# Latent attention scores of a decoder block: from split bf16 stacks to fp32 in four row tiles, with loops written out

## The chip, the cores and the metric

The kernel runs on one core of a Trainium2 chip. The metric is the device time of one execution in microseconds (us). Before the change it is 2980.49 us, the median of 3 runs (2977.54 to 2984.96).

## The reference, cut to what matters

Three layers follow one another on x (4 batches, 1024 rows, 256 columns): a causal self attention (8 heads of 128), a cross attention over 77 context rows (16 heads of 16), and a block with a latent attention (16 heads of 16, keys and values from a 128-wide latent, causal) and a mixture of four experts, one for each row. The change concerns the scores of the latent attention:

```python
q = apply_rope((x @ Wq.T).reshape(b, t, 16, 16).transpose(0, 2, 1, 3))
latent = layernorm(x @ Wdkv.T, ln_g, ln_b)
k = apply_rope((latent @ Wuk.T).reshape(b, t, 16, 16).transpose(0, 2, 1, 3))
v = (latent @ Wuv.T).reshape(b, t, 16, 16).transpose(0, 2, 1, 3)
scores = jnp.einsum('bhqd,bhkd->bhqk', q, k) / np.sqrt(16)
scores = jnp.where(causal, scores, -jnp.inf)
attn = jax.nn.softmax(scores, axis=-1)
out = jnp.einsum('bhqk,bhkd->bhqd', attn, v).transpose(0, 2, 1, 3).reshape(b, t, 256)
```

## The kernel before, in words

Each engine has its own program, written out by hand, and semaphores tie them together. TensorE (PE) does matmuls and transposes into PSUM (8 banks of 512 f32 columns). VectorE (DVE), ScalarE (ACT) and GpSimd (POOL) work on what lies there or in SBUF; GpSimd doesn't read PSUM. SyncE (SP) loads. Every engine loops over the 4 batches (`Fori(0, BATCH)`, PE line 851, DVE 1341, ACT 635, POOL 522, SP 419); inside a batch the self attention loops over pairs of heads (line 962 on PE) and the latent attention over its 4 groups of 4 heads (`Fori(0, NG - 1)`, PE line 1210). After the batches the experts follow (from PE line 1248).

In a batch the order is: self attention, cross attention, and the latent attention, in these steps.

1. Projections. PE multiplies the turned rows by the query and latent weights (line 1088). DVE applies the rotary table to the queries (lines 1489 to 1503), ACT copies the latent columns (713), DVE and POOL normalise them, PE turns them (1095), ACT copies them (717) and PE makes keys and values (1105). DVE rotates the keys (1489 to 1512), ACT copies the values into `mv_rows` (721). While it waits PE runs matmuls of no use, `keep_warm` (823).
2. Stacks. A head has only 16 columns. To get f32 accuracy out of bf16 matmuls, query and key are split into three bf16 parts each, and six products of parts are laid side by side as a contraction of 96 rows (plus 3 rows for the maximum). ACT makes the high parts (736 to 741), DVE splits the queries (1520 to 1525), POOL the keys (557 to 561). PE turns 16 heads x 8 row tiles of each (`turn_stacks`, 1116), DVE (1564) and ACT (750) copy them out. Between the tiles, PE computes the scores of group 0 for its row maxima.
3. Maxima. For each group PE makes the 48 chunks of scores with queries in rows (`max_chunk`, 1127), each up to 512 columns, in a ring of three PSUM banks; a bf16 matmul with the identity adds the causal mask to the 32 chunks on the diagonal (1130). DVE takes the maximum of each chunk (1531). After the last chunk of the group DVE combines and splits the maxima (`stack_max`, 1540 to 1551), PE turns them (`turn_max`, 1138) and DVE and ACT write them into the last rows of the query stack (1555, 758), so that the next matmul subtracts them.
4. Keys. PE makes the scores again with keys in rows (`key_chunk`, 1152, mask 1155), also 48 chunks, in three banks; ACT takes their exponential (773) into `mprobs_t`; PE multiplies by the values (`key_products`, 1167), four heads in four column tiles of 32, f32, into banks 6 and 7; ACT copies a group's output (782). POOL copies the value columns of the group into one tile ahead (567, 572). While the keys of group g run, PE interleaves the maxima chunks of group g + 1, one for one.
5. DVE and POOL normalise the next batch's rows (1318, 1325, POOL 493 to 510), PE turns them (839), and the output projection, the gate and the routing follow.

Other lines named below: 868 and 871 are the output projection of the cross attention (four f32 matmuls of the full array, and the bias as an f32 matmul with one row), 883 the first matmul of a batch, 1365 the row maximum of the self attention.

## Time and profile before

| what | value |
|---|---|
| median of 3 runs | 2980.49 us |
| span of the profiled execution | 2933.7 us, 46553 instructions |
| the profiled execution's own time | not given apart from the runs; the span is 46.8 us under their median |
| PE busy | 2675.2 us (91%) |
| PE weight loads | 1588.7 us (54%) |
| DVE busy | 1476.0 us (50%) |
| ACT busy | 1232.9 us (42%) |
| POOL busy | 335.8 us (11%) |
| mean granted PE clock | 0.967 |

The span runs from the first to the last instruction. "Busy" is the time in which at least one instruction of the engine ran; records of PE overlap one another, as it is a pipeline. An f32 matmul shows as two records, each with its own weight load. "Issue" as a releaser means that the engine waited for nothing that the profile shows.

### The profile page before, as it was taken

To read this page: it belongs to the slowest core of one execution; us is meant where nothing else is said; L and a number is where in the kernel's file an instruction comes from. 1 tells how busy PE (TensorE), PEld (TensorE's weight loads), DVE (VectorE), ACT (ScalarE), POOL (GpSimd) and SP (SyncE) were. 2 spreads that over 40 slices of the span, in tenths; PEclk is the share of its full clock that TensorE was granted. 3 is DMA by queue.
4 is the path that set the end of the run, shared out by engine and by line. 5 is a ranking of instruction groups with operands and counts; after the bars stand their busy time and mean duration, and the time that the engine had idled before them with its cause. 6 is when DMAs were issued, how large, how long until landed. Compare 5 with 4: busy or idle time off the path is not lost.

```text
span 2933.7 us, 46553 instructions
## 1 busy us (share of the span) xinstructions
PE 2675.2 (91%) x14230; PEld 1588.7 (54%) x14303; DVE 1476.0 (50%) x3598; ACT 1232.9 (42%) x2550; POOL 335.8 (11%) x561
## 2 busy tenths in 40 slices
PE   7999997989999987989999988989999978969998
PEld 4565644445656544445556544455566544436775
DVE  3434468754333568743333578734333587632222
ACT  3444225653453425644442435644442445621111
POOL 1000013012000022012000031021000030121111
PEclk9999999999999999999999999989999999979999
DMA  2000000001000000001000000001000000051111
GB/s 92 11 11 1 15 1 1 1 13 41 16 5 1 15 1 1 0 13 46 11 5 1 15 1 1 0 26 33 11 6 15 1 1 1 0 201 51 48 48 34
DMA packets 32401, 58.44 MB, mean 20 GB/s; under 512 B 6980, under 2 KB 23442, under 8 KB 31730
## 3 DMA queue, kind: packets, MB, share of 16 engines
q1 hardware_dynamic: 27490, 43.42, 4.6%
q0 software_dynamic: 4752, 13.02, 1.2%
q8 instruction: 86, 1.41, 0.2%
q14 instruction: 73, 0.60, 0.1%
HBM read 42.09 MB, written 14.32 MB: 19 GB/s over the span
## 4 chain that ended last, share of the span: by engine, by line
issue 78%; PE 11%; POOL 8%; DVE 1%; DMA 1%; POOLq 0%; SPq 0%; ACT 0%; ACTq 0%; DVEq 0%
PE ps L1255 4%; PE ps L1275 4%; POOL tmp L493 2%; PE ps L1264 1%; POOL sorted_rows L593 1%; POOL arena L557 1%; POOL arena L558 1%; POOL arena L559 1%; PE ps L1226 1%; POOL sorted_res L595 1%; POOL scale L493 1%; POOL arena L561 1%; POOL scale L517 1%; PE ps L839 0%; DMA sorted_res<-xres_ids,arena 0%
## 5 line engine op out<-in xcount | busy, mean ns | idle before, releaser
L1365 DVE TENSOR_REDUCE neg_max<-ps 128x1 f32<-128x128 f32 (+7 forms) x256 | 194.1, 758 | 578.9 <-PE ps L913 578.4
L1531 DVE TENSOR_REDUCE arena<-ps 128x1 f32<-128x512 f32 (+3 forms) x768 | 376.9, 550 | 109.6 <-PE ps L1130 50.4
L773 ACT ACTIVATE arena<-ps 128x512 f32<-128x512 f32 (+3 forms) x768 | 320.4, 509 | 156.3 <-PE ps L1155 151.1
L938 PE MATMUL ps<-arena 128*128 128x512 f32 (+3 forms) x768 | 318.0, 501 | 2.0 <-ACT arena L659 1.1
L659 ACT ACTIVATE arena<-ps 128x512 f32<-128x512 f32 (+3 forms) x384 | 188.2, 491 | 290.5 <-PE ps L928 288.5
L910 PE MATMUL ps<-arena 128*128 128x512 f32 (+3 forms) x768 | 290.8, 489 | 4.3 <-ACT arena L668 4.3
L1127 PE MATMUL ps<-arena 128*128 (+4 forms) x708 | 225.1, 327 | 52.6 <-DVE arena L1531 51.3
L1152 PE MATMUL ps<-arena 128*128 (+4 forms) x756 | 240.7, 328 | 12.6 <-ACT arena L758 2.8
L883 PE MATMUL ps<-turned_t,arena 128*128 128x512 f32 x512 | 234.3, 612 | 8.6 <-issue 7.3
L910 PEld LDWEIGHTS ps<-arena 128*128 128x128 f32 x768 | 139.0, 190 | 135.3 <-issue 114.8
L928 PE MATMUL ps<-ident,arena 128*128 128x128 f32 x1152 | 191.6, 276 | 22.6 <-ACT arena L647 13.2
L668 ACT ACTIVATE arena<-ps,neg_max 128x128 f32<-128x128 f32 (+7 forms) x256 | 189.0, 738 | 36.7 <-DVE neg_max L1365 36.6
L928 PEld LDWEIGHTS ps<-ident,arena 128*128 128x128 f32 x1152 | 131.9, 142 | 115.1 <-issue 86.4
L493 POOL TENSOR_TENSOR tmp<-mv,c_eps 128x4 f32<-128x4 f32 x34 | 6.9, 202 | 1509.0 <-DVE mv L1313 1509.0
L883 PEld LDWEIGHTS ps<-turned_t,arena 128*128 128x128 f32 x512 | 97.6, 196 | 122.9 <-issue 122.9
L1152 PEld LDWEIGHTS ps<-arena 128*128 (+1 forms) x768 | 73.4, 97 | 152.9 <-issue 77.0
L823 PE MATMUL ps<-w_out,ident 128*128 128x512 f32 x272 | 152.5, 705 | 0.0
L1127 PEld LDWEIGHTS ps<-arena 128*128 (+1 forms) x768 | 74.4, 97 | 142.0 <-DVE arena L1531 96.0
L643 ACT ACTIVATE arena<-ps 128x512 f32<-128x512 f32 x128 | 76.4, 597 | 175.5 <-PE ps L883 175.5
L1167 PE MATMUL ps<-arena,rows 128*32 128x512 f32 (+3 forms) x1536 | 147.1, 493 | 1.0 <-issue 1.0
L1376 DVE TENSOR_SCALAR arena<-arena,inv_sum 128x128 f32<-128x128 f32 (+7 forms) x256 | 133.6, 522 | 9.1
L938 PEld LDWEIGHTS ps<-arena 128*128 128x128 f32 x768 | 116.0, 191 | 30.4 <-ACT arena L659 27.3
(231 smaller groups left out, 4204.2 us busy)
## 6 DMA issues: line engine op xcount, KB each, us to landing
arena<-in_w_qkv SPq DMA_DIRECT2D x32, 384.0 KB, 3.1
arena<-in_w SPq DMA_DIRECT2D x2, 4096.0 KB, 17.5
xin<-in_x SPq DMA_DIRECT2D x5, 1024.0 KB, 5.3
xres_ids<-sorted_res SPq DMA_DIRECT2D x35, 129.0 KB, 2.2
xin<-sorted_rows SPq DMA_DIRECT2D x35, 128.0 KB, 2.0
mv_rows<-in_b SPq DMA_DIRECT2D x1, 2048.0 KB, 26.7
w_out<-in_w_out SPq DMA_DIRECT2D x1, 1024.0 KB
out<-xin,out_row POOLq DMA_INDIRECT x35, 2.8
```

What stands on the lines that cost most here:

```text
L659: nc.scalar.activation(probs_t[u % 4][:, lo:BANK], ps[:, 4 + u % 2, lo:BANK], ACT.Copy).then_inc(pt_taken, 1)
L668: nc.scalar.activation(probs[par][:, TRI[t]:TRI[t] + n], ps[:, buf:buf + 2, :].rearrange("p a n -> p (a n)")[:, 0:n], ACT.Exp, bias=neg_ma ...
L773: nc.scalar.activation(mprobs_t[kb % 2][:, j, lo:hi], ps[:, 3 + use % 3, 0:hi - lo], ACT.Exp).then_inc(mexp_done, 1)
L823: nc.tensor.matmul(ps[:, bank, :], ident[:], w_out[:, 0:2, :].rearrange("p a n -> p (a n)"), start=True, stop=True)
L883: last = nc.tensor.matmul(ps[:, 4 + i % 3, :], w_head[par][:, kt, w:w + HD], turned_t[:, kt, (i % 2) * BANK:(i % 2 + 1) * BANK], start=(kt ...
L910: last = nc.tensor.matmul(ps[:, buf + c // BANK, 0:m], q_t[par][:, t * P:(t + 1) * P], k_t[par][:, c:c + m], start=True, stop=True)
L928: last = nc.tensor.transpose(ps[:, 4 + u % 2, (t - 4 * g) * P:(t - 4 * g + 1) * P], probs[par][:, TRI[t] + kb * P:TRI[t] + (kb + 1) * P], ...
L938: nc.tensor.matmul(ps[:, 6 + g, lo:BANK], v_rows[par][:, kb, :], probs_t[u % 4][:, lo:BANK], start=(kb == 0), stop=True, skip_group_check= ...
L1127: last = nc.tensor.matmul(ps[:, u % 3, 0:n], q_stack_t[:, head, t * P:(t + 1) * P], k_stack_t[:, head, c * BANK:c * BANK + n], start=True, ...
L1152: last = nc.tensor.matmul(ps[:, 3 + u % 3, 0:hi - lo], k_stack_t[:, head, kb * P:(kb + 1) * P], q_stack_t[:, head, lo:hi], start=True, sto ...
L1365: nc.vector.tensor_reduce(neg_max[:, par, t:t + 1], ps[:, buf:buf + 2, :].rearrange("p a n -> p (a n)")[:, 0:n], AX.X, ALU.max, negate=Tru ...
L1531: nc.vector.tensor_reduce(max_part[:, j, t, c:c + 1], ps[:, u % 3, 0:n], AX.X, ALU.max).then_inc(ms_taken, 1)
```

## The change

The scores of the latent attention are made in f32 instead of from split bf16 parts.

- Queries and keys are rotated straight into slots of 32 columns a head (`q_slots`, `k_slots`), with one extra column in front: 0 in the queries, -1 in the keys. PE turns four heads at once (128 columns) in f32; ACT copies the result (`q_heads_t`, `k_heads_t`). The stacks, their splitting on ACT, DVE and POOL, and their transposes are gone, with all `keep_warm` calls of this attention.
- A score matmul contracts over 17 rows that begin at partition 32 j for head j of the group: four heads lie in four row tiles of the array. The chunks of maxima start with head 2 when the keys start with head 0.
- The causal mask of the maxima is no longer a matmul: DVE reads the scores of a diagonal chunk, adds a constant tile and takes the maximum in one instruction (`tensor_tensor_reduce`). For the keys there is no mask; POOL sets the masked probabilities to 0 after the exponential (`affine_select`, 128 x 4 x 128).
- The maxima of a half group are turned in the ring of the maxima's banks and added by DVE to the extra row of the queries, so that the keys of half 0 can start before the maxima of half 1 are ready.
- Keys now go by items (group, half c, key tile kb): four heads into four banks (3 to 6), in two pairs; ACT takes the exponential of two heads in one instruction. The output of a half uses bank 7 alone. Products come two items after their scores; `mprobs_t` has four buffers. The values are read from `mv_rows` in place, so POOL's copies are gone.
- POOL computes the next batch's scales between the zeroings of half 0 and half 1 of group 3.
- SP waits for the last output copy instead of POOL's last copy before it loads the expert weights.
- The loops over batches, over pairs of heads and over groups are written out (`for` instead of `Fori`); the expert loops stay. The 128x128 bf16 mask constant (32 KB) becomes one of 128x512 f32 (256 KB).

```diff
+    for use in range(2 * NG):
+        n, g = divmod(use, NG)
+        if g == 0:
+            pe.wait_ge(mq_taken, b * NT + 4 * n + 4)
+        if use >= 2:
+            pe.wait_ge(qt_taken, b * (2 * NG) + use - 1)
+        turn_slots(q_slots, g, n, 4 + use % 2).then_inc(qt_done, 1)
...
 def max_chunk(g, i):                                             # PE
+    j, t, c = max_chunk_of(i)
+    slot = chunk_slot(g, i)
     n = min(BANK, (t + 1) * P - c * BANK)
-    if u >= 3:
-        pe.wait_ge(ms_taken, b * (NG * CHUNKS) + g * CHUNKS + u - 2)
-    head = g * GROUP + j
-    last = nc.tensor.matmul(ps[:, u % 3, 0:n], q_stack_t[:, head, t * P:(t + 1) * P],
-                            k_stack_t[:, head, c * BANK:c * BANK + n], start=True, stop=True)
-    if diag:
-        last = nc.tensor.matmul(ps[:, u % 3, n - P:n], ident_b[:], causal_b[:], start=False, stop=True,
-                                skip_group_check=True)
-    last.then_inc(ms_done, 1)
+    if slot >= 3:
+        pe.wait_ge(ms_taken, b * MAX_SLOTS + slot - 2)
+    rows_j = slice(SLOT * j, SLOT * j + MHD + 1)
+    nc.tensor.matmul(ps[:, slot % 3, 0:n], q_heads_t[rows_j, g, t * P:(t + 1) * P],
+                     k_heads_t[rows_j, g, c * BANK:c * BANK + n], start=True, stop=True).then_inc(ms_done, 1)
...
+def item_scores(n):                                              # PE
+    g, c, kb = item_of(n)
+    lo = max(kb * P, c * BANK)
+    hi = (c + 1) * BANK
+    if kb == 0:
+        pe.wait_ge(ms_taken, b * MAX_SLOTS + turn_slot(g, c) + 1)
+    for pair in range(2):
+        if n >= 1:
+            pe.wait_ge(mexp_done, b * (2 * ITEMS) + 2 * n - 1 + pair)
+        for j in range(2 * pair, 2 * pair + 2):
+            rows_j = slice(SLOT * j, SLOT * j + MHD + 1)
+            last = nc.tensor.matmul(ps[:, 3 + j, 0:hi - lo], k_heads_t[rows_j, g, kb * P:(kb + 1) * P],
+                                    q_heads_t[rows_j, g, lo:hi], start=True, stop=True)
+        last.then_inc(mst_done, 1)
+        for i in range(2 * pair, 2 * pair + 2):
+            ahead(g + 1, 4 * HALF * c + 4 * kb + i)
+
+def item_products(n):                                            # PE
...
+    if kb // 4 == c:
+        pe.wait_ge(mdiag_done, b * (NG * NT) + g * NT + kb + 1)
+    pe.wait_ge(mexp_done, b * (2 * ITEMS) + 2 * n + 2)
+    for j in range(GROUP):
+        last = nc.tensor.matmul(ps[SLOT * j:SLOT * (j + 1), 7, lo:BANK], mv_rows[:, kb, GROUP * g + j, :],
+                                mprobs_t[n % BUFS][:, j, lo:BANK], start=(kb == 0), stop=True,
+                                skip_group_check=True)
+    last.then_inc(mpv_done, 1)
...
+for n in range(ITEMS + 2):
+    if n < ITEMS:
+        item_scores(n)
+    if n >= 2:
+        item_products(n - 2)
...
 def max_chunk(g, i):                                             # DVE
+    if c < t // 4:
+        nc.vector.tensor_reduce(part, ps[:, slot % 3, 0:n], AX.X, ALU.max).then_inc(ms_taken, 1)
+    else:
+        nc.vector.tensor_tensor_reduce(max_junk[i % 2][:, 0:n], ps[:, slot % 3, 0:n],
+                                       causal_wide[:, BANK - n:BANK], 1.0, part if c == 1 else MASKED,
+                                       ALU.add, ALU.max, max_stack[:, t, j, 0:1]).then_inc(ms_taken, 1)
...
+                                                                 # ACT
+    nc.scalar.activation(mprobs_t[n % BUFS][:, 2 * pair:2 * pair + 2, lo:BANK],
+                         ps[:, bank:bank + 2, 0:BANK - lo], ACT.Exp).then_inc(mexp_done, 1)
...
+                                                                 # POOL
+    nc.gpsimd.affine_select(mprobs_t[n % BUFS][:, :, at:at + P], mprobs_t[n % BUFS][:, :, at:at + P],
+                            [[0, GROUP], [1, P]], ALU.is_ge, 0.0, base=0,
+                            channel_multiplier=-1).then_inc(mdiag_done, 1)
...
-            with pe.Fori(0, BATCH) as b:
+            for b in range(0, BATCH):
-                with pe.Fori(0, HEADS // 2 - 1) as i:
+                for i in range(0, HEADS // 2 - 1):
```

## Rows read from the trace of the kernel before

**Rows 1.** Stretches of batch 0: length, busy PE, PEld, DVE, ACT, POOL; PEclk, DMA, GB/s.
```profile
421.30:444.50 23.20, 18.26 (x45) 7.35 (x44) 18.93 (x71) 7.67 (x17) 2.88 (x5) 1.00 0.00 0
444.50:499.90 55.40, 38.91 (x350) 27.77 (x354) 48.50 (x93) 28.56 (x39) 23.54 (x34) 0.88 0.01 1
499.90:533.00 33.10, 30.22 (x253) 14.03 (x258) 25.77 (x54) 21.43 (x50) 1.18 (x2) 1.00 0.01 2
533.00:570.80 37.80, 34.94 (x267) 16.52 (x272) 27.12 (x56) 23.35 (x52) 1.18 (x2) 0.95 0.00 0
570.80:608.50 37.70, 34.89 (x266) 16.54 (x270) 27.12 (x56) 23.34 (x52) 1.18 (x2) 0.95 0.00 0
608.50:613.30 4.80, 4.75 (x14) 2.52 (x16) 3.44 (x13) 2.03 (x2) 0.20 (x1) 0.66 0.00 0
613.30:639.90 26.60, 23.79 (x182) 8.48 (x182) 4.14 (x17) 20.37 (x51) 8.51 (x17) 1.00 0.00 1
```
**Rows 2.** Waits of PE, in total, times, longest us.
```profile
PE ps L1127 <- DVE arena L1531: 51.3, 73, 3.1
PE ps L1138 <- DVE arena L1551: 35.0, 16, 2.6
...
PE ps L883 <- issue: 7.3, 3, 2.5
```
**Rows 3.** Timeline of PE in a group turn: start, length.
```profile
505.25 0.38 PE L1127 MATMUL ps<-arena 128*128 x1
505.46 0.22 PE L1130 MATMUL ps<-causal_b,ident_b 128*128 128x128 bf16 x1
505.52 0.33 PE L1152 MATMUL ps<-arena 128*128 x1
```
**Rows 4.** Timeline of PE, f32, and line 1167 from 507.78 to 508.2 us (ns).
```profile
421.26 4.46 PE L823 MATMUL ps<-w_out,ident 128*128 128x512 f32 x10
...
620.20 1.92 PE L1167 MATMUL ps<-arena,rows 128*32 128x512 f32 x16
...
L1167 PE MATMUL ps<-arena,rows x4: 617/617/617, 507.8 to 507.8; 128*32 128x512 f32 x4
```
**Rows 5.** Timelines of PE, ACT and DVE in batch 0.
```profile
402.57 1.09 PE L839 MATMUL ps<-ident,rows 128*128 128x128 f32 x8
...
425.89 0.28 ACT L713 ACTIVATE arena<-ps 128x128 f32<-128x128 f32 x1 [1.03 <-DVE arena L1503]
...
430.30 5.33 PE L1105 MATMUL ps<-mw_kv,arena 128*128 128x512 f32 x12
...
606.14 1.09 ACT L782 ACTIVATE arena<-ps 128x512 f32 x2 [1.11 <-PE ps L1167]
...
36.15 0.29 DVE L1365 TENSOR_REDUCE neg_max<-ps 128x1 f32<-128x128 f32 x1 [13.82 <-PE ps L913]
```
**Rows 6.** The costliest groups: busy us, mean ns, idle before.
```profile
L1531 DVE TENSOR_REDUCE arena<-ps 128x1 f32<-128x512 f32 (+3 forms) x768 | 376.9, 550 | 109.6 <-PE ps L1130 50.4
```
**Rows 7.** Timeline of PE in the cross attention's output projection.
```profile
399.20 1.13 PE L868 MATMUL ps<-xw_o,turned_t 128*128 128x256 f32 x4
400.26 0.69 PE L871 MATMUL ps<-bo,ones_f 1*128 1x256 f32 x2
400.88 1.13 PE L868 MATMUL ps<-xw_o,turned_t 128*128 128x256 f32 x4
```
**Rows 8.** Timeline of POOL.
```profile
476.21 0.73 POOL L561 TENSOR_TENSOR arena<-arena 128x256 bf16<-128x256 f32 x1
...
606.22 1.04 POOL L572 COPY rows<-mv_rows 128x1024 f32 x1
...
613.10 0.20 POOL L493 TENSOR_TENSOR tmp<-mv,c_eps 128x4 f32<-128x4 f32 x1 [5.84 <-DVE mv L1313]
...
622.85 0.20 POOL L510 TENSOR_TENSOR scale<-tmp,c_root 128x4 f32<-128x4 f32 x1
```

More of the change, by code:

```diff
@@ L62, in norm_count, with max_chunk_of, chunk_slot, turn_slot @@
     return b * (2 * NORMS) + 2 * use + half + 1
-MAX_CHUNKS = [(j, t, c) for j in range(GROUP) for t in range(NT) for c in range(t // 4 + 1)]
-FIRST_CHUNKS = sorted(MAX_CHUNKS, key=lambda x: (x[1], x[0], x[2]))
-CHUNKS = len(MAX_CHUNKS)
+CHUNKS = 48
+MAX_SLOTS = NG * (CHUNKS + 2)
+ITEMS = NG * 3 * HALF
+BUFS = 4
+def max_chunk_of(i):
+    j = (i + 2) % GROUP
+    if i < 4 * HALF:
+        return j, i // GROUP, 0
+    return j, HALF + (i - 4 * HALF) // (2 * GROUP), (i // GROUP) % 2
+def chunk_slot(g, i):
+    return (CHUNKS + 2) * g + i + (g > 0 and i >= 4) + (i >= 20) - (g > 0)
+def turn_slot(g, half):
+    return chunk_slot(g, 20) - 1 if half == 0 else \
+        (chunk_slot(g + 1, 4) - 1 if g + 1 < NG else MAX_SLOTS - 1)
+def item_of(n):
+    g, i = divmod(n, 3 * HALF)
+    return (g, 0, i) if i < HALF else (g, 1, i - HALF)
 class Count:
@@ L417, in batch_io @@
                 sp.wait_ge(turn_done, b * (4 * TURNS) + 4 * TURN_NEXT + 4)
-            with sp.Fori(0, BATCH - 1) as b:
-                batch_io(b, sp.snap(b * T + T))
+            for b in range(0, BATCH - 1):
+                batch_io(b, b * T + T)
                 load_head(0, 0)
@@ L579, in _ @@
+                for g in range(NG):
+                    keep_causal(g)
                 for h in range(2):
@@ L633, in _ @@
             turn_copy(0, TURN_SELF, turned_t, gamma)
-            with act.Fori(0, BATCH) as b:
+            for b in range(0, BATCH):
                 def take_qkv(h, par):
@@ L849, in _ @@
             pe.wait_ge(turn_taken, 4 * TURN_SELF + 4)
-            with pe.Fori(0, BATCH) as b:
+            for b in range(0, BATCH):
                 def turn(use):
@@ L961, in _ @@
                 project_v(1, 1)
-                with pe.Fori(0, HEADS // 2 - 1) as i:
+                for i in range(0, HEADS // 2 - 1):
                     for u in range(2):
@@ new lines, in turn_max @@
+                def turn_max(g, half):
+                    slot = turn_slot(g, half)
+                    pe.wait_ge(ms_taken, b * MAX_SLOTS + (slot if g == NG - 1 and half == 1 else slot - 2))
+                    for t in range(4 * half, 4 * half + 4):
+                        last = nc.tensor.transpose(ps[:, slot % 3, (t % 4) * P:(t % 4 + 1) * P],
+                                                   max_stack[:, t, :, :].rearrange("p j e -> p (j e)"), ident[:])
+                    last.then_inc(ms_done, 1)
@@ new lines, in ahead @@
+                def ahead(g, i):
+                    if g < NG:
+                        max_chunk(g, i)
+                        if i == 19:
+                            turn_max(g, 0)
+                        if i == 3 and g > 0:
+                            turn_max(g - 1, 1)
+                    elif i == 3:
+                        turn_max(g - 1, 1)
+                def item_scores(n):
+                    g, c, kb = item_of(n)
+                    lo = max(kb * P, c * BANK)
+                    hi = (c + 1) * BANK
+                    if kb == 0:
+                        pe.wait_ge(ms_taken, b * MAX_SLOTS + turn_slot(g, c) + 1)
+                    for pair in range(2):
+                        if n >= 1:
[7 more added lines that the diff above has]
+                            ahead(g + 1, 4 * HALF * c + 4 * kb + i)
@@ L1339, in _ @@
             dve.wait_ge(dve_step, first())
-            with dve.Fori(0, BATCH) as b:
+            for b in range(0, BATCH):
                 step = Count(b * DVE_STEPS + first.n)
@@ L1399, in _ @@
                 head(0, 0, None)
-                with dve.Fori(0, HEADS // 2 - 1) as i:
+                for i in range(0, HEADS // 2 - 1):
                     for u in range(2):
@@ new lines, in take_max @@
+                def take_max(g, half):
+                    slot = turn_slot(g, half)
+                    dve.wait_ge(ms_done, b * MAX_SLOTS + slot + 1)
+                    q_half = q_heads_t[:, g, half * BANK:(half + 1) * BANK]
+                    nc.vector.tensor_tensor(q_half, q_half, ps[:, slot % 3, :], ALU.add).then_inc(ms_taken, 1)
+                dve.wait_ge(slots_made, b * 3 + 3)
+                for g in range(NG):
+                    for i in range(CHUNKS):
+                        max_chunk(g, i)
+                        if i == 3 and g > 0:
+                            take_max(g - 1, 1)
+                        if i == 19:
+                            take_max(g, 0)
@@ L1575, in _ @@
+                take_max(NG - 1, 1)
                 dve.wait_ge(x_in, b * 16 + 32)
```

391 lines of the change are left out of this document (118 added, 273 removed).

## The prediction, made before the change was run

> **What bounds the kernel now.** I read the page first: TensorE (PE) is busy 91% of 2933.7 us, no other engine over 50%. Its chain of waits runs along GpSimd (POOL), mostly as "issue", and says nothing here. So I went by stretches of one batch [rows 1]. The change lives in 421.3 to 639.9 us, 218.6 us of a batch's 650. There are four pieces: 23.2 us of projections, 55.4 us in which the bf16 stacks are built, turned, and the maxima of head group 0 found, three group turns (33.1 + 37.8 + 37.7 + 4.8 = 113.4 us, so 37.8 a group), and a last group without maxima ahead, 26.6 us. In the second piece PE is busy 38.9 of 55.4 us and VectorE (DVE) 48.5: DVE sets it. In a group turn PE is busy 34.9 of 37.8, and the only long stall is the hand-over of the maxima, 2.6 us, where PE waits for DVE line 1551 [rows 2].
>
> A group turn checks out by pace. A bf16 matmul of 512 columns takes 0.21 us to the next start, and a mask matmul 0.06 [rows 3]. A group has 96 score chunks, 384 columns on average: 96 x 0.16 = 15.4 us. With 64 masks (3.5) and the value products (7.7, below) that is 26.6 us; 16 changes of the array's shape at some 0.15 (below) give 29, and the hand-over with its warm matmuls 5 to 6 more.
>
> **The price of an f32 matmul.** Five warm f32 matmuls of 512 columns show as 10 records in 4.46 us [rows 4]: two records of 0.43 us each, 0.86 us a matmul, four times the bf16 one. The change pays by width: a head uses 17 rows of the array, and four heads lie in four row tiles. The trace has no row tile of f32 with company. It has column tiles: 8 products of 512 columns, 16 records, take 1.92 us [rows 4], that is (1.92 - 0.59)/3 = 0.44 us per four records, and four records start within 0.03 us. So four column tiles run fully together. If row tiles do too, a score chunk costs 0.86/4 = 0.21 us at 512 columns, exactly the bf16 price.
>
> **Part 1, projections (23.2 us): +1.** The 8 query turns now sit ahead of the latent turn. ScalarE (ACT) reaches their copies after its last latent copy (425.89 + 0.28) [rows 5]; 8 copies in a ring of two banks, each 0.45 (four turns on PE, eight take 1.09) + 0.17 (what a record shows beyond its streaming) + 0.54 (ACT, half of 1.09 for two) + 0.1, over 2, so 0.65 us, end at 431.4 [rows 5]. The key-value matmuls had started at 430.30 [rows 5]; they start some 2 us later, and everything behind them with them. The stretch before ended in 2 us of waiting for the first split rows, which go, and the first key turn takes 1: +1. The ten warm matmuls go too, and PE idles some 4 us while ACT gets to its copies: +1.5 for a clock at half speed for a while, as each hand-over shows it (0.95 in two stretches [rows 1]). Bounds 0 and +5.
>
> **Part 2, maxima of group 0 (55.4 us): 30.** Gone are 256 bf16 transposes, the splitting on ACT, DVE and POOL, 32 mask matmuls. What is left is DVE's 48 chunks: 376.9/768 = 0.49 us each [rows 6] = 23.6 us. 32 of them become an add-and-maximum with a mask tile; no such operation is in the trace. Lower bound: 0.1 below the plain reduction, since its last step into a shared tile goes; upper: +0.4 us each, about one more pass over their mean 320 columns. I take +0.05, nearest to the row that reads the same PSUM columns: 1.6 us. Two additions of 512 columns at 0.6: 1.2. Three PSUM banks circulate; with 0.86 us instead of 0.21 for the matmul, a 512-column chunk goes round in 0.53 + 0.86 + 0.17 + 0.2 over 3 = 0.59 against 0.55: 2. Start and key copies 1.6. Sum 30: a gain of 25.4.
>
> **Part 3, three group turns.** In one of the 12 items of a group PE issues two rounds, each two key chunks and two chunks of maxima, in four different row tiles. A round lasts as long as its longer pair: over 12 items these lengths add up to 5760 columns; two rounds at 1.67 ns a column: 19.2 us. Products 4608 columns x 1.67 ns: 7.7. Shape changes: between full-array and one-row f32 matmuls a tile of the output projection takes 1.69 us (399.20 to 400.88) [rows 7], of which 4 x 0.214 + 2 x 0.214 = 1.28 is streaming: 0.2 each, with a 128-column weight load exposed. The change has 24 a group, half of them with 32-column loads: 24 x 0.15 = 3.6. Two turns of the maxima (four transposes and a shape change each) 1.5. That is 32.0, if no wait falls on PE. One does: the fourth maxima chunk of an item uses the bank of the first, which ended one round (0.86) earlier and still needs 0.17 + 0.69 on DVE. That is 0.85 us in each of the 6 items with 512-column maxima and 0.6 in two more: 6.3. Sum 38.3 against 37.8: the hand-over that goes is paid back by this. Three turns +1.5; bounds 32.0 and, with heads overlapping only in pairs, 43.5 (rival 1).
>
> **Part 4, last group (26.6 us): 27.5.** Without company keys run 1.28 us per 512-column item (three staggered records) and products 0.86: 9 x 2.14 = 19.3, plus 24 x 0.15 = 3.6 and the end of the chain, some 4: +1.
>
> **POOL, moved steps and queues.** The causal zeroing, 8 of 128 x 512 elements a group, is new on POOL. It lies between the exponential and a product that is issued two items (4 us or more) later. Nearest rows: a copy of 1024 elements, 1.04 us, and additions of 256 at 0.73 [rows 8]; 0.5 to 2 us, hidden. Beyond 4 us it would set the last group. POOL's scales for the next batch (613.10 to 623.05, 10 us) now stand between the 4th and 5th zeroing of group 3; the 5th is due some 19 us into that group, the scales start at 9: just hidden. Value columns are read in place, so POOL's four copies go. SP's wait moves to the last output copy, but its next wait, unchanged, is later. The wide mask is 224 KB more to load at the start, with 13.8 us in which DVE has its constants and waits for PE [rows 5].
>
> **Part 5, loops written out.** The first matmul of a new batch (line 883) waits up to 2.5 us with no releaser, 7.3 us in three times [rows 2]: -7.3. Other loop ends leave no such wait on PE. Bounds 0, if code that runs straight on waits as long for its next block, and -12, if the inner loops' register work also cost something. The Trainium skill, "Runtime: NRT & Kernel Launch", Instruction fetch mechanics, says that a taken branch breaks sequential prefetch; by that rule these stalls go, and the trace agrees.
>
> **Sum.** Per batch +1 + 1.5 - 25.4 + 1.5 + 1 = -20.4. Four batches: -82, loops -7: -89. The profiled execution has a span of 2933.7 us; its own total isn't given, so I lay the 46.8 us between span and the median of the three runs (2980.5) around it, and the sum then stands against the median itself: 2891. Forecast 2890.
>
> **Rivals.**
> 1. *Passes stay in order.* Each maxima matmul has its own wait and signal. If its second record must start before the next tile's first, a round lasts key + 3 x maxima records: 18432 columns in total, 15.4 us a round set, 30.7 for two, + 7.7 + 3.6 + 1.5 = 43.5 a turn, +17.1 in three. Per batch -5.5, total -29: 2951. For it: in rows 4 nothing waits between the four. Against: those four records already run ahead of each matmul's own second. The skill's "TensorE: Matmul & The Clock Gate", Part 3, says matmuls are never reordered; by that rule this is the case. Chance 0.23.
> 2. *The masked maximum is dear.* At +0.4 us, 32 chunks: +11 in part 2 and some +3 a turn (DVE then has 37 of 38 us): +20 a batch, 2970. Nothing in the rows speaks for it. Chance 0.11.
> 3. *Row tiles hardly overlap (slower).* Place: the score rounds. Score work unshared is 96 x 0.64 = 61.4 us a turn and 30.7 in the last group; at an overlap c of 2 or less a batch takes about 24 + 31 + 3 x (61.4/c + 13) + 30.7/c + 11, against 218.6. Break-even is c = 1.9. At 1.7 it is +13 a batch, 3024; at 1.5, +30, 3092; at 1, +101, 3378. A granted clock that stays at its lower level, 1.2 GHz, through the turns acts the same way. For it: no row shows a row tile in company. Against: column tiles reach 4. Chance 0.18, half of it with c between 1.9 and 1.7.
> 4. *It does not do what it says.* The four row tiles are written but some wait in DVE's or POOL's order (the first maxima of a half, the zeroing) eats what part 2 gives: within 9 us of before. For it: PE is in order, and every wait holds the score rounds too. Chance 0.06.
>
> **Numbers.** The forecast case has 0.42; each rival as given. Its own range is 2825 (turns of 32 us) to 2925. A measurement tells 0.3%, 9 us, from no change. Faster: 0.42, 0.8 of rival 1, 0.8 of rival 2: 0.69. Same 0.09, slower 0.22. The range runs from 2830 to 3010: it leaves out the far end of rival 3 and little below.
>
> **What would show it.** Right: the stretch from the last key-value matmul to the first key chunk near 30 us; group turns near 38 with no 2.6 us hand-over; four MATMUL records of score lines starting within 0.05 us; no "issue" wait ahead of the first matmul of a batch. Wrong: second records of maxima matmuls before the next tile's first (rival 1), masked maxima over 0.8 us at 512 columns (2), a granted clock near 0.5 across group turns, or score rounds near 1.7 us or more (3), products waiting for POOL.

## The result, and the profile after

The changed kernel takes 3371.07 us (median of 4 runs, 3369.1 to 3372.03) against 2979.59 for the kernel before, run beside it: ratio 1.1315, 95% interval 1.1301 to 1.1328. The forecast was 2890, in a range of 2830 to 3010. It was wrong in sign and by 481 us.

The page of the changed kernel: busy PE, then PE's busy tenths and the granted clock in 40 slices of the 3370.3 us span.

```profile
PE 3168.7 (94%) x13862; PEld 1743.0 (52%) x13863; DVE 1394.1 (41%) x3854; ACT 1104.4 (33%) x2038; POOL 298.9 (9%) x513
...
PE   7999989998999989998999989998999989996998
...
PEclk9999965568999965568999965568999965567999
```

Four valleys of 5 and 6 stand in the clock, one for each batch's latent attention; PE is as busy there as elsewhere. The stretches of batch 0, columns as in [rows 1]: projections, maxima of group 0, three group turns, last group.

```profile
419.60:446.00 26.40, 17.79 (x75) 11.44 (x73) 17.57 (x68) 11.40 (x24) 2.43 (x4) 0.84 0.00 1
446.00:487.40 41.40, 39.65 (x117) 23.81 (x118) 25.84 (x77) 2.99 (x5) 0.00 (x0) 0.54 0.00 1
487.40:557.10 69.70, 68.65 (x287) 27.93 (x283) 29.50 (x88) 19.72 (x25) 5.11 (x8) 0.50 0.00 1
557.10:627.90 70.80, 69.77 (x303) 27.41 (x300) 27.75 (x82) 20.31 (x26) 5.10 (x8) 0.50 0.00 1
627.90:698.70 70.80, 69.77 (x303) 27.41 (x299) 27.77 (x82) 20.31 (x26) 5.10 (x8) 0.50 0.00 1
698.70:740.70 42.00, 41.55 (x217) 12.04 (x214) 6.80 (x27) 19.23 (x26) 13.82 (x26) 0.50 0.00 1
```

In [rows 1] the same work had a granted clock of 0.88 to 1.00, but for 4.8 us at 0.66; here it is 0.50, the lower of the two levels, 1.2 GHz, in all turns. PE is busy 69.77 of 70.80 us, DVE 27.75: nothing but PE's pace sets the turn. The six stretches sum to 321.1 us against 218.6, so +102.5 a batch, +410 in four; the written-out loops give some 10 of it back between the stages (below). Are row tiles at fault? The timeline of PE:

```profile
524.28 1.08 PE L1154 MATMUL ps<-arena,mv_rows 128*32 128x512 f32 x4
525.29 1.22 PE L1138 MATMUL ps<-arena 17*128 17x512 f32 x2
525.30 1.22 PE L1103 MATMUL ps<-arena 17*128 17x256 f32 x4
526.30 1.08 PE L1138 MATMUL ps<-arena 17*128 17x512 f32 x4
```

No: two key matmuls (L1138, once L1152) and two maxima matmuls (L1103, once L1127) start within 0.02 us, in four tiles. An f32 matmul shows as two records, called its passes below. The second records don't keep the program's order either: those of L1103 (256 columns) start at 525.89, those of L1138 (512 columns), issued earlier, at 526.30.

### The profile page after: what moved, and what is told of

It is laid out like the page before. It is cut to its first block, busy times and chain, and to the rows that moved or that the text cites. A ratio compares the mean times of both kernels' runs of the same rounds, so it can differ in the third digit from the quotient of the medians.

```text
span 3370.3 us, 38347 instructions
## 1 busy us (share of the span) xinstructions
PE 3168.7 (94%) x13862; PEld 1743.0 (52%) x13863; DVE 1394.1 (41%) x3854; ACT 1104.4 (33%) x2038; POOL 298.9 (9%) x513
## 4 chain that ended last, share of the span: by engine, by line
PE 75%; DVE 5%; issue 2%; ACT 2%; POOL 1%; another core or an unknown queue 1%; SPq 0%; DMA 0%; DVEq 0%; ACTq 0%; POOLq 0%
PE ps L1103 15%; PE ps L1138 9%; PE ps L1154 8%; PE ps L900 6%; PE ps L872 6%; PE ps L845 5%; PE ps L1217 4%; PE ps L1237 4%; PE ps L830 3%; PE ps L890 3%; PE ps L855 2%; PE ps L992 2%; PE ps L1010 1%; PE ps L1056 1%; PE ps L1111 1%
## 5 line engine op out<-in xcount | busy, mean ns | idle before, releaser
L1103 PE MATMUL ps<-arena 17*128 17x512 f32 (+3 forms) x1536 | 723.5, 902 | 19.5 <-DVE arena L1494 14.4
L739 ACT ACTIVATE arena<-ps 128x1024 f32<-128x1024 f32 (+3 forms) x384 | 302.5, 809 | 779.9 <-PE ps L1138 779.4
L1138 PE MATMUL ps<-arena 17*128 17x512 f32 (+3 forms) x1536 | 479.8, 876 | 2.7 <-ACT arena L739 2.7
L1103 PEld LDWEIGHTS ps<-arena 17*128 17x128 f32 x1536 | 315.7, 310 | 219.1 <-DVE arena L1494 80.5
L1138 PEld LDWEIGHTS ps<-arena 17*128 17x128 f32 x1536 | 200.7, 312 | 260.1 <-issue 173.9
L872 PE MATMUL ps<-arena 128*128 128x512 f32 (+3 forms) x768 | 304.5, 508 | 26.4 <-ACT arena L661 16.0
L652 ACT ACTIVATE arena<-ps 128x512 f32<-128x512 f32 (+3 forms) x384 | 188.2, 491 | 297.1 <-PE ps L890 295.1
L1154 PE MATMUL ps<-arena,mv_rows 128*32 128x512 f32 (+3 forms) x1536 | 284.7, 838 | 0.3 <-POOL arena L562 0.3
L1489 DVE TENSOR_REDUCE arena<-ps 128x1 f32<-128x512 f32 x256 | 169.5, 688 | 218.0 <-PE ps L1103 218.0
L872 PEld LDWEIGHTS ps<-arena 128*128 128x128 f32 x768 | 143.7, 197 | 165.1 <-issue 135.0
L1494 DVE CUSTOM_DVE_ANT_0 arena<-ps,causal_wide,arena 128x128 f32<-128x128 f32 (+3 forms) x256 | 133.9, 549 | 186.7 <-PE ps L1103 146.8
L1494 DVE CUSTOM_DVE_ANT_0 arena<-ps,causal_wide 128x128 f32<-128x128 f32 (+3 forms) x256 | 118.7, 490 | 159.2 <-PE ps L1103 157.6
L562 POOL TENSOR_SCALAR_AFFINE_SELECT arena<-arena 128x512 f32<-128x512 f32 x128 | 81.6, 638 | 1123.3 <-ACT arena L739 1123.3
```

The costliest lines, as they stand in the source:

```text
L652: nc.scalar.activation(probs_t[u % 4][:, lo:BANK], ps[:, 4 + u % 2, lo:BANK], ACT.Copy).then_inc(pt_taken, 1)
L739: nc.scalar.activation(mprobs_t[n % BUFS][:, 2 * pair:2 * pair + 2, lo:BANK], ps[:, bank:bank + 2, 0:BANK - lo], ACT.Exp).then_inc(mexp_do ...
L872: last = nc.tensor.matmul(ps[:, buf + c // BANK, 0:m], q_t[par][:, t * P:(t + 1) * P], k_t[par][:, c:c + m], start=True, stop=True)
L1103: nc.tensor.matmul(ps[:, slot % 3, 0:n], q_heads_t[rows_j, g, t * P:(t + 1) * P], k_heads_t[rows_j, g, c * BANK:c * BANK + n], start=True, ...
L1138: last = nc.tensor.matmul(ps[:, 3 + j, 0:hi - lo], k_heads_t[rows_j, g, kb * P:(kb + 1) * P], q_heads_t[rows_j, g, lo:hi], start=True, sto ...
L1154: last = nc.tensor.matmul(ps[SLOT * j:SLOT * (j + 1), 7, lo:BANK], mv_rows[:, kb, GROUP * g + j, :], mprobs_t[n % BUFS][:, j, lo:BANK], st ...
```

## The experiments

Thirteen versions ran, three of them twice, and the two unchanged kernels again, on six chips. On three of them the kernel before takes 2934 to 2939 us (e1 to e4, e14 to e18), on the three others 2979 (e5 to e13), as beside the changed kernel's first runs; what differs there is told at the end of this section. "Stages" is the sum over four batches from the first latent projection to the last value product, from the records; for the kernel before it is 915.1 us. Single runs have no interval.

| run | ratio to before | interval | mean clock | stages, us |
|---|---|---|---|---|
| changed kernel | 1.1315 | 1.1301 to 1.1328 | 0.805 | 1320.6 |
| e5 matmuls of no use ahead of the stage | 1.132 | one run | 0.813 | 1326.8 |
| e2 / e18 32 rows | 1.0135 / 1.0113 | 1.0110 to 1.0159 / 1.0094 to 1.0132 | 0.945 / 0.943 | 959.7 / 958.1 |
| e10 24 rows | 1.078 | one run | 0.865 | 1160.1 |
| e3 full-array matmul per item | 1.1071 | 1.1036 to 1.1106 | 0.907 | 1262.5 |
| e4 bf16, 17 rows | 1.0519 | 1.0501 to 1.0537 | 0.876 | 1066.2 |
| e1 / e16 loops only | 0.9933 / 0.9915 | 0.9910 to 0.9956 / 0.9898 to 0.9931 | 0.970 / 0.967 | 901.0 / 906.4 |
| e11 same tiles | 1.040 | one run | 0.930 | 1047.4 |
| e6 plain maximum | 1.0057 | 1.0038 to 1.0076 | 0.939 | 955.7 |
| e7 late fourth chunk | 1.0025 | 1.0007 to 1.0043 | 0.941 | 935.1 |
| e8 dense matmuls among the maxima | 1.0141 | 1.0114 to 1.0168 | 0.957 | 982.1 |
| e9 turns among the maxima | 1.0278 | 1.0264 to 1.0292 | 0.919 | 1008.5 |
| e12 ring of four | 0.9944 | 0.9932 to 0.9957 | 0.943 | 909.1 |
| e13 / e17 and late query turns | 0.9885 / 0.9864 | 0.9870 to 0.9899 / 0.9842 to 0.9885 | 0.948 / 0.957 | 889.5 / 884.6 |
| e14 before / e15 changed, again | 1.001 / 1.137 | one run each | 0.966 / 0.807 | 914.4 / 1326.4 |

### Is it the clock, and what lowers it?

The theories: A, too few of the array's rows at work; B, the clock is lost in the gaps ahead of the stage, where matmuls of no use had stood; C, f32 or row tiles as such, whatever their rows.

**e2, 32 rows instead of 17.** The added rows are zero in both operands, so the same products are summed; the waits for `slots_made` count the two new memsets.

```diff
+nc.gpsimd.memset(q_slots[:, :, :, MHD + 1:SLOT], 0.0).then_inc(slots_made, 1)
+nc.gpsimd.memset(k_slots[:, :, :, MHD + 1:SLOT], 0.0).then_inc(slots_made, 1)
-rows_j = slice(SLOT * j, SLOT * j + MHD + 1)
+rows_j = slice(SLOT * j, SLOT * (j + 1))
```

> The changed kernel, each head's score matmul contracting over the 32 rows of its tile (rows 17 to 31 are zeroed by GpSimd) instead of 17. Four heads then use 128 rows, not 68. Theory A (the clock falls because few rows of the array are at work): granted clock back near 1 in the group turns, a turn from 70 to about 38 us, in all some 2850 to 2900. Theory B (it falls in the gaps ahead of the stage, with the matmuls of no use gone, and does not climb again) and theory C (row tiles or f32 score matmuls themselves, whatever rows they have): 3371 within 10, clock 0.5 through the stage. Part way: one tile of 32 rows still counts as few when it runs with one other.

Measured: 2973.28 us, ratio 1.0135, still slower than the kernel before. Theory A's 2850 to 2900 was too low all the same: a turn takes 42.4 us and not 38, and the clock is not back at once. Stretches of batch 0, from group 0's maxima on:

```profile
447.60:487.50 39.90, 38.22 (x116) 22.21 (x117) 25.59 (x76) 3.23 (x6) 0.00 (x0) 0.59 0.00 1
487.50:535.50 48.00, 45.47 (x284) 20.76 (x280) 28.72 (x87) 19.17 (x25) 5.09 (x8) 0.84 0.00 1
535.50:578.00 42.50, 39.44 (x304) 16.37 (x300) 27.14 (x83) 19.66 (x26) 5.08 (x8) 1.00 0.00 1
578.00:620.40 42.40, 39.35 (x300) 16.27 (x297) 27.05 (x83) 19.66 (x26) 5.08 (x8) 1.00 0.00 1
620.40:648.00 27.60, 26.75 (x217) 8.99 (x214) 6.98 (x29) 19.02 (x26) 13.77 (x26) 1.00 0.00 1
```

A turn falls from 70.8 to 42.4 us and the last group from 42.0 to 27.6, with the clock at 1.00, 2.4 GHz. Group 0's maxima, which have three banks and so three tiles at work, stay at 0.59, and the first turn has 0.84. B and C fall: no matmul was added ahead of the stage, where PE has one wait more, of 3.2 us (next paragraph), and the matmuls are still f32 in four row tiles.

One thing ahead of the stage did change, and it costs time. POOL's two memsets (L550, L551) come while DVE normalises rows, and the DVE instruction that runs beside them ends only when they do: 4.90 us in e2, 1.63 in the changed kernel with its shorter memsets, 0.40 for those behind it.

```profile
408.80 1.63 DVE L1439 TENSOR_SCALAR xp<-xres_ids,mv,scale 128x256 f32<-128x256 f32 x1
...
408.81 4.90 DVE L1441 TENSOR_SCALAR xp<-xres_ids,mv,scale 128x256 f32<-128x256 f32 x1
410.23 1.70 POOL L550 MEMSET arena<- 128x1920 f32 x1
411.87 1.70 POOL L551 MEMSET arena<- 128x1920 f32 x1
417.41 7.09 PE L1052 MATMUL ps<-mw_qd,turned_t 128*128 128x384 f32 x16 [3.18 <-ACT arena L708]
```

The first line is the changed kernel's, the others are e2's. The rotation of the queries starts 3.3 us later, and PE waits 3.18 us amid the latent projections. The first maxima chunk comes 38.7 to 40.4 us after the first projection, for 36.9 to 37.1 in the changed kernel: some 11 us in four batches. Every version built on e2 carries this; zeros written at another place were not tried.

**e10, 24 rows.**

```diff
-rows_j = slice(SLOT * j, SLOT * (j + 1))
+rows_j = slice(SLOT * j, SLOT * j + 24)
```

> The 32-row version with a contraction of 24 rows a head (96 rows of the array at most, between 68 and 128). Theory A (what counts is how much of the array's rows work): a clock between, or one of the two ends: at 0.5 throughout, ratio 1.13; at 1 in the turns, 1.01; switching between both, 1.03 to 1.10. Nothing but a dependence on rows gives a value other than the 32-row version's.

```profile
493.70:563.40 69.70, 68.65 (x286) 27.92 (x282) 29.56 (x88) 19.73 (x25) 5.11 (x8) 0.50 0.00 1
563.40:618.60 55.20, 52.90 (x304) 22.11 (x300) 27.41 (x82) 19.89 (x26) 5.10 (x8) 0.72 0.00 1
618.60:679.60 61.00, 59.21 (x303) 24.40 (x300) 27.40 (x81) 20.09 (x26) 5.10 (x8) 0.62 0.00 1
```

Three turns of the same work, at a clock that goes to and fro. Over all four batches the turns have 0.50 to 0.91 and take 46 to 71 us. That lies between the two ends, as A alone has it.

**e5, the matmuls of no use put back.** `keep_warm(5, 7)` ahead of the query turns and of the key turns, `keep_warm(4, 3)` ahead of the first keys.

> The changed kernel (17 rows a head) with matmuls of no use as the kernel before had them: 5 ahead of the query turns, 5 ahead of the key turns, 4 ahead of the first keys. Theory B (the clock is lost in the gaps ahead of the stage): granted clock back near 1 through the group turns, 3371 down to some 2870. Theory A (few rows at work): the clock is 1 for some microseconds and 0.5 in all four groups again; time as the changed kernel, ratio to before 1.13, plus or minus 10 us.

```profile
495.00:500.90 5.90, 5.69 (x51) 4.02 (x50) 3.81 (x20) 4.06 (x5) 1.28 (x2) 1.00 0.00 0
500.90:560.20 59.30, 58.27 (x232) 20.47 (x230) 24.03 (x65) 15.58 (x20) 3.82 (x6) 0.50 0.00 1
560.20:631.00 70.80, 69.77 (x300) 27.43 (x296) 27.75 (x82) 20.34 (x26) 5.09 (x8) 0.50 0.00 1
```

The first keys start at 495.0 with the full clock, and 5.9 us into the turn it is gone, while PE is busy nearly all the time. B is refuted a second time. The ratio, 1.132, is what A expected.

**e4, the old bf16 stacks with 17 rows.** Based on e1; it leaves out the lower parts of the split, the subtraction of the maximum and the causal mask.

```diff
-last = nc.tensor.matmul(ps[:, u % 3, 0:n], q_stack_t[:, head, t * P:(t + 1) * P],
-                        k_stack_t[:, head, c * BANK:c * BANK + n], start=True, stop=True)
+last = nc.tensor.matmul(ps[:, u % 3, 0:n], q_stack_t[0:17, head, t * P:(t + 1) * P],
+                        k_stack_t[0:17, head, c * BANK:c * BANK + n], start=True, stop=True)
```

> The kernel before (loops written out) with its bf16 score matmuls contracting over rows 0 to 16 of the stacks instead of all, and without the mask matmuls; it leaves out the lower parts of the split, the subtraction of the maximum and the causal mask. One row tile, full-width columns. Theory A (few rows): granted clock near 0.5 in the group turns and a turn of about 50 us or more: 3050 to 3250. Theory C (f32 or row tiles): clock near 1, the masks' 64 x 0.06 us a group gone: 2973 - 16 x 4 = about 2910. Theory B: as C, since its keep-warm matmuls are there.

```profile
500.00:546.00 46.00, 43.87 (x204) 13.98 (x204) 27.76 (x56) 24.18 (x53) 1.20 (x2) 0.63 0.00 1
546.00:589.00 43.00, 39.94 (x207) 13.16 (x206) 27.27 (x56) 23.32 (x52) 1.18 (x2) 0.74 0.00 1
589.00:638.00 49.00, 47.03 (x206) 15.17 (x205) 28.27 (x57) 24.05 (x52) 1.21 (x2) 0.60 0.00 1
```

Less work, and slower: turns of 43 to 49 us where e1 with all rows takes 32.5 in the first and 37.0 in the second. Neither f32 nor row tiles are needed to lose the clock. How much of the loss is due to the 17 rows and how much to the 128-row mask matmuls, which are gone too, this version does not tell apart.

**e3, dense work added.** One f32 matmul of 128 rows and 512 columns ahead of each item, 17-row scores kept.

> The changed kernel with one f32 matmul of 128 rows and 512 columns, of no use, ahead of each item's first pair of scores (48 a batch, into a bank that the scores then overwrite). At full clock they cost 0.86 us each, 41 a batch; at half clock 1.72, 83 a batch. Theory A: their density decides; if they hold the clock up, a turn takes about 38 + 10 = 48 us and the whole 3371 - 4 x (130 - 41) = about 3015. Theory B: the clock climbs once and stays: same 3015. Theory C, or A with too little dense work: clock stays 0.5 and the time rises to about 3371 + 330 = 3700.

```profile
560.30:621.70 61.40, 58.34 (x321) 20.83 (x320) 27.20 (x82) 19.67 (x26) 5.10 (x8) 0.89 0.00 1
```

The clock goes up to 0.89, a turn from 70.8 to 61.4 us (in the last batch 0.74 and 71 us); the matmuls themselves, 10.3 us a turn at full clock by the expectation's 0.86, and the time at the lower level eat most of it. 3256.58 us lies between the two numbers expected. Zero rows (e2) beat added matmuls.

### Do four row tiles work together?

**e11, maxima in the tiles of the keys beside them,** on the 32-row version: `j = i % GROUP` for `j = (i + 2) % GROUP`.

> The 32-row version with the maxima chunks in the same row tiles as the keys of their pair (heads 0, 1 beside 0, 1) in place of the other two. If row tiles are independent of each other, as the records of the changed kernel look, and one tile serves one matmul at a time: a round takes two turns of 0.86 us in place of one, up to 19 us a turn more, less what the bank wait already cost (5): +14 x 3 x 4 = 170 us, ratio 1.07. If overlap never came from the tiles: no change, 1.0135. The clock may fall too, with half the rows at work at a time: then ratio 1.10 or more.

```profile
621.75 1.15 PE L1140 MATMUL ps<-arena 32*128 32x512 f32 x8
622.72 0.62 PE L1105 MATMUL ps<-arena 32*128 32x256 f32 x6
623.99 0.69 PE L1105 MATMUL ps<-arena 32*128 32x256 f32 x2 [0.65 <-DVE arena L1496]
```

Now all four heads' keys (L1140) run first, together, and three maxima together after them. The program has two keys, two maxima, two keys, two maxima: the second pair of keys started ahead of maxima that were issued before it. So a tile takes one matmul at a time, and the tiles run ahead of one another. A turn at clock 0.98 takes 48.7 us against 42.4. The +14 expected was misworked: each tile has one key and one maxima chunk an item in either version, so the work of a tile is the same. What the row shows as lost is 0.65 us of waiting for a bank by the fourth maxima chunk, against 0.13 us in e2's row below; how the 6 us a turn are made up beyond that is not shown.

### The rest of the gap: 42 us a turn for 38, 40 us of maxima for 30

**e6, plain maximum.** It leaves the causal mask out of the maxima.

> The 32-row version (ratio 1.0135) with a plain row maximum in place of the masked one; it leaves the causal mask out of the maxima (not out of the probabilities). If the masked maximum costs little, as forecast (0.05 us of 32 chunks a group): 2973 less 5 to 10 us, and a turn stays at 42.4 us. Rival 2 (the masked maximum is dear, in its extra wait on the chunk before or in its time): a turn falls by 3 us or more, in all 40 to 60 us less, ratio to before near 0.995.

A turn takes 42.0 us instead of 42.4, the stages 955.7 instead of 959.7: the masked maximum costs about 1 us a batch. That is 0.0014 of the ratio; 1.0057 is lower than e2's 1.0135 by more. The two ran on different chips (below), and that this makes the rest is likely but not shown: e2 itself did not run on a slower one.

**e7, the fourth chunk behind the products.**

```diff
-for i in range(2 * pair, 2 * pair + 2):
+for i in range(2 * pair, min(2 * pair + 2, 3)):
     ahead(g + 1, 4 * HALF * c + 4 * kb + i)
...
     item_products(n - 2)
+if n < ITEMS:
+    g, c, kb = item_of(n)
+    ahead(g + 1, 4 * HALF * c + 4 * kb + 3)
```

> The 32-row version with the fourth chunk of maxima of each item issued behind the item's products instead of ahead of them. The forecast put 6.3 us a turn on its wait for the bank that the first chunk of the item used. If that is so, 3 x 6.3 x 4 = 75 us less at most, 2900 on a chip where the 32-row version takes 2973; since the chunk now runs beside the next item's first keys only in part, I expect half: 2935. If the wait is hidden anyway: no change, 2973; if VectorE bounds the turn, no change either.

Expected were 38 us less than e2; the stages have 24.6 less. A turn takes 41.0, 1.5 us less and not 6.3; the first turn 43.1 instead of 48.0, as the clock came back 5 us earlier (over the four batches 43.0 to 44.7 instead of 45.0 to 48.0). What the wait had cost is seen in e2's timeline:

```profile
521.38 0.59 PE L1105 MATMUL ps<-arena 32*128 32x512 f32 x1
521.39 0.59 PE L1140 MATMUL ps<-arena 32*128 32x512 f32 x2
521.95 1.12 PE L1105 MATMUL ps<-arena 32*128 32x512 f32 x2
523.00 1.06 PE L1156 MATMUL ps<-arena,mv_rows 128*32 128x512 f32 x8
```

The wait is short: the round's last pass starts at 521.39 and takes 0.43, so the array is free at 521.82 and the chunk starts at 521.95. The larger cost is that it then runs alone: 1.05 us until the products start at 523.00. Together that is 1.18 us, where the forecast had 0.85. Behind the products it has one key beside it (e7's records start together at 555.69), but holds up the other, whose tile it uses.

**e8, dense work among the maxima of group 0:** the matmuls of no use of e5, and four bf16 matmuls of 128 x 128 behind every second chunk.

> The 32-row version with matmuls of no use ahead of query turns, key turns and first keys, and, in the maxima of group 0, four bf16 matmuls of 128 rows and 128 columns after every second chunk (24 times 0.25 us). In the 32-row version the granted clock is 0.59 in these 40 us. Theory A (maxima alone keep one or two tiles of 32 rows at work): the dense matmuls lift the clock to near 1 and the stretch falls from 40 to about 30 us, DVE's pace: in all 2973 - 4 x 8 = 2940. If DVE sets the stretch at either clock: 2973 or a little more.

```profile
449.90:503.00 53.10, 53.10 (x221) 25.80 (x220) 26.46 (x81) 3.25 (x6) 0.00 (x0) 0.68 0.00 1
```

Expected were 32 us less than e2; the ratio is 1.0141. The stretch grows from 40 to 53 us though the clock rises to 0.68; the first turn, at full clock, falls only from 48.0 to 41.2. **e9** does the like with useful work: on top of e7, one query or key turn behind every fourth chunk.

> The version with the late fourth chunk (ratio to before 1.0025), with the query and key turns of groups 1 to 3 (12 of 16) taken out of the projections and set one behind every fourth chunk of group 0's maxima. Forecast: the latent turn no longer waits for query copies (3 us a batch), the 12 key turns leave the path to the first chunk (1 us), and full-array work among the chunks may lift the granted clock of that stretch from 0.5 (up to 8 us a batch). Ratio 0.998 if the clock stays, down to 0.987 if it rises. If PE bounds that stretch at half clock, the moved turns are paid there: ratio 1.002 to 1.006.

```profile
471.64 0.63 PE L1065 MATMUL ps<-ident,arena 128*128 128x128 f32 x2
472.20 2.08 PE L1111 MATMUL ps<-arena 32*128 32x512 f32 x6
475.06 2.07 PE L1111 MATMUL ps<-arena 32*128 32x512 f32 x2 [0.77 <-DVE arena L1500]
477.06 1.11 PE L1065 MATMUL ps<-ident,arena 128*128 128x128 f32 x4
```

A miss, with its reason in view. Three chunks run together in 2.08 us (half clock), the fourth waits for a bank and then takes 2.07 alone, and the full-array turn behind it (L1065) starts only when it is done. That beat costs 61.4 us for the 40. But the first chunk did start 5 us earlier (444.5 against 449.8 in e7).

**e12, four banks for group 0's maxima,** on top of e7:

```diff
+def max_bank(slot):
+    return slot % 4 if slot < RING4 else (slot - RING4) % 3
```

with waits to match, bank 3 being free until the first keys (`RING4 = 44`).

> The version with the late fourth chunk (ratio 1.0025), with a ring of four banks instead of three for the maxima of group 0, so that four row tiles, 128 rows, can be at work there. If TensorE's pace with three tiles at half clock bounds the stretch: four 512-column chunks take 2.08 us even at half clock, VectorE needs 2.75, so VectorE sets it: from 40 to some 30 us, 10 us a batch, ratio 0.989; and the granted clock of the stretch goes above 0.6. If VectorE or its hand-over bounds it already: 1.0025 within 0.002.

```profile
446.10:477.40 31.30, 29.68 (x117) 20.02 (x118) 24.18 (x77) 3.22 (x6) 0.00 (x0) 0.67 0.00 1
477.40:522.90 45.50, 44.47 (x284) 21.06 (x280) 28.02 (x83) 18.86 (x25) 5.11 (x8) 0.85 0.00 1
522.90:563.80 40.90, 39.79 (x299) 17.73 (x296) 27.10 (x83) 19.04 (x26) 5.10 (x8) 1.00 0.00 1
```

31.3 us for 40.0: three banks, and so three tiles, at nearly half clock had been the bound, not DVE. The first turn pays 2.4 us of it back (45.5 for 43.1), so the stages fall by 6.5 us a batch and the ratio is 0.9944 for the 0.989 expected. **e13** moves the query turns of groups 1 to 3 behind the key-value matmuls.

> As the ring of four, and the query turns of groups 1 to 3 behind the key-value matmuls instead of ahead of the latent turn. The turns among the chunks gave a first chunk 3 to 5 us earlier, of which the key turns had 2.5; so 2 to 3 us a batch here: ratio 0.003 to 0.004 below the ring of four alone. If the rotation of the keys on VectorE takes up the time won (it starts when the first key-value matmul ends, so it should not): no change.

5 us a batch less again (stages 889.5 against 909.1), more than the 2 to 3 expected. With 2942.53 us against 2978.75 this version beats both kernels.

### The loops, and the chip

**e1, the kernel before with its loops written out.**

> The kernel before with only its loops over batches, pairs of heads and groups written out. Forecast (part 5): 7 us faster, 2973, with the wait of up to 2.5 us with no releaser ahead of the first matmul of a batch gone. Rival: straight code waits for its own instructions elsewhere (the changed kernel has such waits of up to 4.3 us ahead of self attention scores and 12 us on ScalarE): 2980 to 3000. Theory that the clock is at fault: nothing of it here, granted clock 0.97 in the mean.

22.7 us faster. The waits of [rows 2] ahead of line 883, 7.3 us, are gone; but a group turn also falls from 37.8 to 37.0 and the self attention between two stages by 3 us, so inner loops had a price too.

**e14, e15, the two kernels again, profiled on one chip.**

> The kernel before, unchanged, profiled beside the changed kernel. If the 12 us a batch between two latent stages belong to the chip: where the kernel before is timed at 2979, its own profile has a span near 2977 and 429 to 431 us from the last value product of a batch to the next batch's latent projections; where it is timed at 2936, span 2934 and 419. If they belong to the changed code: 419 us here whatever the time, and 46 us lie outside the span.

> The changed kernel, unchanged, in the same call. Chip's: the stretch between two latent stages is 3 us shorter than the kernel before has in this call (the loops), 416 or 427. Code's: 12 us a batch longer than the kernel before has in this call. The latent stage takes 331 us a batch and clock 0.5 either way.

Chips differ. Here the kernel before took 2936.49 us, with a span of 2934.5, and the changed kernel 3336.46; between two stages they take 419 and 416 us, where the changed kernel's first profile has 429, with these waits of PE ahead of the self attention scores:

```profile
PE ps L872 <- ACT arena L661: 16.0, 9, 3.9
...
PE ps L872 <- issue: 10.4, 6, 4.3
```

against these in e15:

```profile
PE ps L872 <- ACT arena L661: 4.4, 12, 0.4
```

Those 12 to 13 us a batch are the chip's, not the change's: every version profiled where the kernel before takes 2979 (e5 to e13) has 424 to 431 us between two stages, every one where it takes 2934 to 2939 has 413 to 422. The kernel before itself has no profile on a slower chip. What makes those chips wait stays open.

**e16, e17, e18: the versions whose comparison crossed chips, on one chip.**

> The kernel before with its loops written out, again, beside e17. By its latent stages (901 us in four batches against 915) and the stretches between them (3 us each): 22 to 24 us below the kernel before, ratio 0.992 to 0.9935 on either chip.

> The ring of four with late query turns, again. By its latent stages (889.5 us against 901 in the loops version) it should be 11 us below e16 in the same call, ratio 0.988 to 0.990. If the slow stretches of the self attention hit written-out code less than looped code on the other chip, and that made its 0.9885: equal to e16 here within 3 us.

> The 32-row version, again. On the chip where the kernel before takes 2936: ratio 1.0135 as before. On the one where it takes 2979: 1.009 to 1.0135; then the clock gives back 0.118 to 0.1225 there.

2914.61, 2897.78 and 2972.44 us beside 2939.0: the ring of four with late query turns is 16.8 us faster than the loops alone (2893 to 2904 against 2910 to 2920; 11 expected). The changed kernel did not run on this chip; on e15's, where the kernel before takes the same within 0.2%, 17 rows stand at 1.137, against 1.0113 for 32 rows here. So the rows alone are worth 0.126, some 369 us, with the cost of the memsets in it.

## Why the prediction was wrong, point by point

**The step that failed: part 3, "two rounds at 1.67 ns a column", with "Products 4608 columns x 1.67 ns" beside it.** That pace came from full-array matmuls and column tiles [rows 4], at a granted clock near 1, and I carried it to row tiles of 17 rows. The experiments put the loss on the rows: 17 rows had a granted clock of 0.50 in the turns, 32 rows 1.00 from the second turn on (e2), with everything else in the turn alike. At 0.50 the streaming doubles. The sum has 19.2 + 7.7 = 26.9 us of it in a turn, and 70.8 us is 28.4 more than e2's 42.4; the last group has 42.0 for e2's 27.6. Nothing in the trace of before had few rows in dense use, so the pace had no bound, and I treated it as known.

**Rival 3** had, in one sentence, the right mechanism ("A granted clock that stays at its lower level, 1.2 GHz, through the turns acts the same way"), but without a price of its own. Its 3378, so near the 3371 measured, is the price of c = 1, no overlap at all, four times the score work's streaming. That is luck: halving c from 4 to 2, as half a clock does to the scores, gives 212.5 us a batch in its own formula, below the 218.6 of before, since it leaves products and the maxima of group 0 as they are. Its main mechanism, tiles that don't overlap, was wrong, and c below 1.7 had a chance of 0.09. The clock deserved a rival of its own with a price: the change sets 68 rows at most where the stacks' matmuls had 128 [rows 3]. The Trainium skill, "TensorE: Matmul & The Clock Gate", Part 1, What's actually happening, says that the clock is set by how busy TensorE has been recently. The trace here does not bear that out as it stands: PE was busy 69.77 of 70.80 us and had half the clock.

**Rival 1 fell.** Passes overtake one another across tiles, as the timeline of the changed kernel shows. The Trainium skill, "TensorE: Matmul & The Clock Gate", Part 3, says that matmuls are never reordered. For row tiles the traces here disagree: second passes of 256 columns start at 525.89, ahead of those of 512 columns issued earlier at 526.30, and in e11 whole key matmuls start ahead of maxima issued before them. Its sum had a slip: 17.1 in three turns gives -4.8 a batch and 2954, not -5.5 and 2951. **Rival 4** did not come in.

**Part 1, +2.5:** right in the changed kernel, 26.4 for 25.7. That the query turns stand in the way was right too; moving six of the eight gave 5 us a batch (e13), of which some 3 are in group 0's maxima (in the mean of the batches 29.4 us for 32.4).

**Part 2, 30:** wrong, 41.4, and 39.9 even with 32 rows. I took DVE as the bound at full clock. With three banks, and so three tiles, the clock stayed near half (0.54 and 0.59) and PE set it; with four banks it is 31.3.

**Part 3 at full clock:** 38.3 forecast, 42.4 in e2, inside its bounds. The fourth chunk was seen, but as a wait on DVE (0.85 us an item, 6.3 a turn); in e2's row it costs 1.18, of which 1.05 is that it runs alone. The first pass of that item takes 0.53 us for 0.43. The rest of the 4.1 us was not taken apart. The sum by which this pace was to give the group turn of before does not close either: 29 and 5 to 6 us are 34 to 35, some 3 short of 37.8.

**Part 4:** 27.5 forecast; 42.0, and 27.6 at full clock. **Masked maximum, rival 2:** fell, about 1 us a batch. **POOL:** the zeroing of probabilities is hidden, POOL busy 5.10 us a turn; no matmul of PE waits over 0.3 us for it in e2 (1.2 us in all), weight loads up to 0.8. That POOL's memsets hold up a DVE instruction was not in the forecast (e2). **Part 5:** -7.3 forecast, -22.7 and -24.4 measured, beyond the bound of -12.

**The sum against the median:** the 46.8 us "between span and median" don't lie around the span; 2 us do. The rest is that the kernel was timed on a chip on which it is slower than on the one of the profile.

## What to carry to other kernels

Before packing a small contraction into row tiles, ask what granted clock matmuls of that kind have in a trace: 17-row tiles ran at 1.2 GHz here however busy PE was, and filling the contraction to 32 rows with zeros gave 0.126 of the time back, for two memsets that hold DVE up by 3.3 us a batch where they stand. Give a ring as many banks as there are tiles (40.0 us to 31.3), and keep full-array work out of a tiled stretch (40.0 us to 61.4). Written-out loops were worth 0.7% and 0.9% here, another chip 1.5%: differences of that size ask for runs on one chip.

## What was not expected of the hardware

- The granted clock depended on how many rows contract, and rows of zeros counted: in the group turns 0.50 with 17 rows, 0.50 to 0.91 with 24, and 1.00 with 32, of which 15 are zero, once past the first turn (0.84). For bf16 in one tile, 17 rows gave 0.60 to 0.74, with the 128-row masks gone too.
- With 17 rows the clock fell and stayed low while PE was 98% busy (e5), after dense work had brought it to full.
- A DVE instruction of 0.40 us took 4.90 us, to the end of the POOL memsets beside it (e2).
- Row tiles act like four separate queues: in e11 four keys issued in pairs, with maxima between the pairs, started together.
- Chips differ by 1.5% for the kernel before (2936 and 2979) and by 1.0% for the changed one (3336 and 3371); for the latter the profiles put it into the stretch between two latent stages, three times 12 to 13 us.
